# Attention of a two-layer kernel: scores made twice in 32-row tiles, the second time with the keys on partitions, against scores made once and transposed

## What is computed

```
q = (x @ wq).reshape(B, T, 2, 4, 128);  k_lat, v_lat = x @ wk_down, x @ wv_down      # 32 latent features a kv head
k = einsum('bkhl,ld->bkhd', k_lat, wk_up);  v = einsum('bkhl,ld->bkhd', v_lat, wv_up)
scores = einsum('bqhrd,bkhd->bhrqk', q, k) * scale
scores = where(causal, scores, lowest)
y = einsum('bhrqk,bkhd->bqhrd', softmax(scores), v)
out = y.reshape(B, T, 1024) @ wo
```

## Time and profile before

| | us |
|---|---|
| median of 3 runs | 2718.06 (2718.0 to 2718.55) |
| span of the profiled execution, first to last instruction | 2716.9 |
| PE busy in that span | 2138.8 (79%) |
| DVE busy | 1699.1 (63%) |
| ACT busy | 1440.2 (53%) |
| POOL busy | 1094.3 (40%) |
| mean granted TensorE clock | 0.861 |

### The profile page before, as it was taken

The page is one execution under the profiler, slowest core; times in us unless marked ns, Lnnn a source line. Parts: engine busy times, 40 slices in busy tenths (PEclk is TensorE's granted clock), DMA queues, the critical chain, the costliest instruction groups (busy, mean ns, idle before and its releaser), DMA issues.

```text
span 2716.9 us, 30658 instructions
## 1 busy us (share of the span) xinstructions
PE 2138.8 (79%) x8216; PEld 931.0 (34%) x8216; DVE 1699.1 (63%) x2749; ACT 1440.2 (53%) x2340; POOL 1094.3 (40%) x934
## 2 busy tenths in 40 slices
PE   5667887788778887788877888788877878778777
PEld 1201233343334333343333433333333433334344
DVE  1886458754688347882688646884477835877143
ACT  3342755647555565646556465554655556554352
POOL 0453146523465135550455323652346513554031
PEclk9556898898889987898888988889888989789898
DMA  5000000001000010000000000000100000000000
GB/s 162 15 20 8 12 12 13 16 6 24 1 13 16 6 24 12 17 5 12 12 13 16 6 15 9 13 16 6 24 5 17 8 8 21 13 13 5 0 1 4
DMA packets 55270, 41.95 MB, mean 15 GB/s; under 512 B 12672, under 2 KB 53264, under 8 KB 55056
## 3 DMA queue, kind: packets, MB, share of 16 engines
q1 hardware_dynamic: 50832, 37.41, 5.7%
q10 hardware_dynamic: 4224, 2.10, 0.3%
HBM read 12.21 MB, written 2.10 MB: 5 GB/s over the span
## 4 chain that ended last, share of the span: by engine, by line
PE 42%; issue 21%; DVE 20%; ACT 10%; POOL 5%; DVEq 1%; SPq 1%; ACTq 0%; POOLq 0%; DMA 0%
PE ps_g L636 15%; DVE sb_hst L1084 8%; PE ps_att L636 5%; PE ps_dt L540 5%; PE ps_y L587 4%; DVE sb_dbu L1077 3%; POOL sb_hc L1307 3%; PE ps_g L721 2%; POOL sb_h L1321 2%; PE ps_dt L575 2%; PE ps_du L540 2%; PE ps_g L713 2%; PE ps_att L733 2%; PE ps_du L569 1%; DVE sb_nmax L1195 1%
## 5 line engine op out<-in xcount | busy, mean ns | idle before, releaser
L1307 POOL TENSOR_TENSOR sb_hc<-sb_hst,sb_crep 128x512 f32<-128x512 f32 x512 | 654.2, 1279 | 743.5 <-DVE sb_hst L1084 743.5
L1084 DVE TENSOR_TENSOR_SCAN sb_hst<-ps_dt,sb_dbu 128x512 f32<-128x512 f32 x512 | 620.8, 1213 | 2.8 <-ACT ps_dt L854 1.4
L854 ACT ACTIVATE ps_dt<-ps_dt,sb_A 128x512 f32<-128x512 f32 x512 | 334.8, 660 | 404.6 <-PE ps_dt L575 403.1
L1077 DVE TENSOR_TENSOR sb_dbu<-ps_du,sb_brep 128x512 f32<-128x512 f32 x512 | 350.6, 685 | 233.5 <-PE ps_du L569 226.4
L575 PE MATMUL ps_dt<-sb_stk,sb_sel 96*128 96x512 bf16 x512 | 224.1, 438 | 100.4 <-DVE sb_hst L1084 97.3
L931 ACT ACTIVATE sb_h<-ps_g,sb_nmax 128x128 f32<-128x128 f32 (+3 forms) x256 | 134.8, 527 | 294.1 <-DVE sb_nmax L1195 262.0
L569 PE MATMUL ps_du<-sb_stk,sb_sel 96*128 96x512 bf16 x512 | 223.3, 436 | 68.1 <-DVE sb_dbu L1077 54.1
L1321 POOL TENSOR_TENSOR sb_h<-sb_h,sb_rz 128x128 f32<-128x128 f32 (+3 forms) x256 | 190.3, 746 | 185.4 <-DVE sb_rz L1199 173.1
L713 PE MATMUL ps_g<-sb_g,sb_qz 128*128 128x512 f32 (+3 forms) x512 | 222.2, 521 | 37.2 <-DVE sb_qz L1186 34.7
L1289 POOL TENSOR_TENSOR sb_tser<-sb_tser,sb_texp 128x512 f32<-128x512 f32 x32 | 40.5, 1265 | 495.5 <-ACT sb_tser L814 495.5
L721 PE MATMUL ps_g<-sb_const,sb_h 128*128 128x128 f32 x640 | 141.4, 326 | 122.5 <-POOL sb_h L1321 88.9
(11 more groups left out here) (249 smaller groups left out, 3594.3 us busy)
## 6 DMA issues: line engine op xcount, KB each, us to landing
sb_stk<-sb_parts SPq DMA_DIRECT2D x384, 64.0 KB, 2.0
sb_xtok<-in_L_attn_x_dram SPq DMA_DIRECT2D x8, 256.0 KB, 3.2
sb_ew<-in_L_ffn_w_dram SPq DMA_DIRECT2D x2, 1024.0 KB, 8.0
out_dram<-sb_lnv ACTq DMA_DIRECT2D x8, 256.0 KB, 2.5
sb_h<-in_L_ffn_h_w_dram SPq DMA_DIRECT2D x1, 1024.0 KB, 7.5
sb_g<-in_L_ffn_h_w_dram SPq DMA_DIRECT2D x1, 1024.0 KB, 8.8
sb_ew<-in_L_ffn_w_dram SPq DMA_DIRECT2D x8, 128.0 KB, 5.0
sb_hc<-in_L_attn_fw_convw_dram SPq DMA_DIRECT2D x1, 512.0 KB
```

The source lines that it names most:

```text
L854: act.activation(ps_dt[n % 2][:], ps_dt[n % 2][:], ACT.Exp, scale=A[d][:, g:g + 1]).then_inc(sem["dA"], 1)
L1077: dve.tensor_tensor(dbu[:, n % 2, :], ps_du[:], brep[n // NU][:], ALU.mult).then_inc(sem["dbu"], 1)
L1084: dve.tensor_tensor_scan(hst[:, n % 3, :], ps_dt[n % 2][:], dbu[:, n % 2, :], 0.0, ALU.mult, ALU.add).then_inc(sem["scan"], 1)
L1307: pool.tensor_tensor(hc[:, n % 6, :], hst[:, n % 3, :], crep[n // NU][:], ALU.mult).then_inc(sem["hc"], 1)
```

## The change

The head-by-head attention is replaced by one that works on pairs of heads, in two passes per sequence.

- **First pass**, 16 steps `s0` to `s15` (kv head, query tile t, pair): PE makes the scores of two heads, each a product over 32 rows (row tiles that start at partition 0, 32, 64 or 96), into the two banks of one pair of banks, and adds the mask to both. DVE takes the two heads' maxima in one reduction of 2x(t+1)*128 columns. The pairs of banks take turns. There is no `qz`, no exponential. After each eighth pair DVE splits the negated maxima into three bf16 parts (4 small operations on 128x16, `split`).
- **Between**, step `mT`: PE transposes the parts (4 bf16 transposes), ACT copies them to SBUF.
- **Second pass**, steps i = 0 to 17: for pair `e_i` (kv head, key tile j, pair) PE makes the scores again, with 128 keys on partitions and the (4-j)*128 queries along the row, two 32-row tiles; adds the negated maxima by a bf16 product over 32 rows (`pick`), and the mask. ACT makes one exponential of both heads, straight to SBUF. It is the operand of the values: no transposes, no copies. One step later `values(i-1)` makes, in four 32-column tiles, two products with `vlat` and two with a matrix of ones, which give the sums (`ps_z`). All `e_i` use the same pair of banks; `ps_att` and `ps_z` hold the other pair.
- **Normalisation** once per kv head (steps i = 9 and 17): ACT makes two Ln of 64 rows of `ps_z` and one Exp of the negative, DVE multiplies `ps_att` by it into `yT`. POOL has no part in the attention any more.
- `COST` gets entries for the new steps, so `FOLLOW` changes. The steps are 35 as before (26 to 60). Step 21 moves from slot 12 to 13. Slots 17 to 25 now hold s0,s1,s2 | s3,s4 | s5 | s6 | s7,s8,s9 | s10,s11 | s12,s13 | s14 | s15,mT, and slots 26 to 40 hold i = 0 | none | 1 | 2 | 3,4 | 5 | 6,7 | 8 | 9 | 10 | 11 | 12 | 13,14 | 15,16 | 17 with "ao" and its variance (these two were in slot 41).

```diff
+PAIRS = KV * TT * (REP // 2)
+def pair(i):
+    return i // (TT * REP // 2), i // (REP // 2) % TT, i % (REP // 2)
...
 PE:
+                def scores(i):
+                    k, t, p = pair(i)
+                    claim(f"s{i}")
+                    o = ps_pair[i % 2]
...
+                    for h, rows in heads(p):
+                        pe.matmul(o[:, h, 0:(t + 1) * P], qT[rows, k, t * P:(t + 1) * P], kT[rows, k, 0:(t + 1) * P],
+                                  start=True, stop=False)
+                    for h, _ in heads(p):
+                        ins = pe.matmul(o[:, h, t * P:(t + 1) * P], identb[:], maskb[:], start=False, stop=True)
+                def turned_scores(i):
+                    k, j, p = pair(i)
+                    claim(f"e{i}")
+                    o = ps_pair[0]
...
+                    for h, rows in heads(p):
+                        pe.matmul(o[:, h, j * P:T], kT[rows, k, j * P:(j + 1) * P], qT[rows, k, j * P:T],
+                                  start=True, stop=False)
+                    for h, rows in heads(p):
+                        pe.matmul(o[:, h, j * P:T], pick[rows, k, :], mT[rows, j * P:T], start=False, stop=False)
+                    for h, _ in heads(p):
+                        ins = pe.matmul(o[:, h, j * P:(j + 1) * P], maskb[:], identb[:], start=False, stop=True)
+                def values(i):
+                    k, j, p = pair(i)
+                    if i % (PAIRS // 2) == 0:
+                        claim(f"att{k}")
...
+                    for h, rows in heads(p):
+                        pe.matmul(ps_att[rows, j * P:T], vlat[:, j, k * LAT:(k + 1) * LAT],
+                                  pexp[i % 4][:, h, j * P:T], start=(j == 0), stop=(j == TT - 1))
+                    for h, _ in heads(1 - p):
+                        other = slice(LAT * (2 * (1 - p) + h), LAT * (2 * (1 - p) + h + 1))
+                        ins = pe.matmul(ps_z[other, j * P:T], ones[:], pexp[i % 4][:, h, j * P:T],
+                                        start=(j == 0), stop=(j == TT - 1))
+                for i in range(PAIRS):
+                    scores(i)
+                    yield
+                o = claim("mT")[:, 0:T // 2].bitcast(BF16)
+                pe.wait_ge(sem["split"], row("split", 2))
+                for t in range(TT):
+                    ins = pe.transpose(o[:, t * P:(t + 1) * P], nsplit[:, t, :, :].rearrange("p r c -> p (r c)"), identb[:])
+                for i in range(PAIRS + 2):
+                    if i < PAIRS:
+                        turned_scores(i)
+                    if 1 <= i <= PAIRS:
+                        values(i - 1)
+                    yield
...
 ACT:
+                act.activation(mT, full("mT")[:, 0:T // 2].bitcast(BF16), ACT.Copy).then_inc(sem["mT"], 1)
+                for i in range(PAIRS + 2):
+                    if i < PAIRS:
+                        act.activation(pexp[i % 4][:, :, j * P:T], ps_pair[0][:, :, j * P:T], ACT.Exp
+                                       ).then_inc(sem["pexp"], 1)
+                    if i in (PAIRS // 2 + 1, PAIRS + 1):
+                        k = pair(i - 2)[0]
+                        act.wait_ge(sem["att"], row("att", PAIRS // 2 * (k + 1)))
+                        for rows, other in ((slice(0, P // 2), slice(P // 2, P)), (slice(P // 2, P), slice(0, P // 2))):
+                            act.activation(logz[rows, :], ps_z[other, :], ACT.Ln).then_inc(sem["logz"], 1)
+                        act.wait_ge(sem["logz"], row("logz", 2 * k + 2))
+                        act.activation(rz[:], logz[:], ACT.Exp, scale=-1.0).then_inc(sem["rz"], 1)
...
 DVE:
+                    dve.tensor_reduce(nmax[:, k, t, 2 * p:2 * p + 2], ps_pair[i % 2][:, :, 0:(t + 1) * P], AX.X, ALU.max,
+                                      negate=True).then_inc(sem["smax"], 1)
+                    if i % (PAIRS // 2) == PAIRS // 2 - 1:
+                        split(k)
...
+                    if i in (PAIRS // 2 + 1, PAIRS + 1):
+                        dve.wait_ge(sem["rz"], row("rz", k + 1))
+                        dve.tensor_tensor(yT[:, k, :], ps_att, rz[:], ALU.mult).then_inc(sem["yT"], 1)
...
 COST:
-..., att0=0.9, att1=0.62, ...
+..., s0=0.7, s1=0.5, e0=1.2, e1=0.7, ...
-    rest += [w["att0"] + w["att1"] * head(min(j, HEADS * TT - 1))[1] for j in range(HEADS * TT + 3)]
+    rest += [w["s0"] + w["s1"] * pair(i)[1] for i in range(PAIRS)] + [w["ln"]]
+    rest += [w["e0"] + w["e1"] * (TT - 1 - pair(min(i, PAIRS - 1))[1]) for i in range(PAIRS + 2)]
```

More of the change, by code:

```diff
@@ L157, in rest_uses, with place @@
     return uses
-def place(uses, bank_of, before):
+def place(uses, banks_of, before):
     placed, last, i = {}, dict(before), 0
     for name, semaphore, count in uses:
-        bank = bank_of(i, name)
-        placed[name] = (bank, last[bank], i)
-        last[bank] = (semaphore, count)
+        banks = banks_of(i, name)
+        placed[name] = (banks, list(dict.fromkeys(last[bank] for bank in banks)), i)
+        last.update({bank: (semaphore, count) for bank in banks})
         i += name[:3] not in ("att", "sum")
@@ L383, in two_layer_kernel @@
         block = ctx.enter_context(nc.Block())
-        turn_banks = [bank[name] for name in ("g0", "g1", "g2", "att")]
+        turn_banks = [bank[f"g{i}"] for i in range(4)]
         def use(name):
-            return bank[(M_USE if name in M_USE else R_USE)[name][0]]
+            return bank[(M_USE if name in M_USE else R_USE)[name][0][0]]
         def first(name):
@@ L624, in claim @@
                 def claim(name):
-                    pe.wait_ge(sem[R_USE[name][1][0]], row(*R_USE[name][1]))
+                    for freed in R_USE[name][1]:
+                        pe.wait_ge(sem[freed[0]], row(*freed))
                     return use(name)
@@ L705, in rest, with heads @@
                 yield
+                def heads(p):
+                    return ((h, slice(LAT * (2 * p + h), LAT * (2 * p + h + 1))) for h in range(2))
                 def scores(i):
-                    k, t, r = head(i)
-                    o = claim(f"s{i}")
-                    if t == 0 and r == 0:
-                        pe.wait_ge(sem["kT"], row("kT", k + 1))
-                    pe.wait_ge(sem["qz"], row("qz", i + 1))
-                    pe.matmul(o[:, 0:(t + 1) * P], qz[:, r, :], kT[:, k, 0:(t + 1) * P], start=True, stop=False)
@@ L736, in values @@
[L736 to L744 removed]
+                    pe.wait_ge(sem["pexp"], row("pexp", i + 1))
+                    for h, rows in heads(p):
+                        pe.matmul(ps_att[rows, j * P:T], vlat[:, j, k * LAT:(k + 1) * LAT],
+                                  pexp[i % 4][:, h, j * P:T], start=(j == 0), stop=(j == TT - 1))
@@ new lines, in split @@
+                def split(k):
+                    m = nmax[:, k, :, :]
+                    hi, mid, lo = (nsplit[:, :, :, 2 * part + k] for part in range(3))
+                    dve.wait_ge(sem["smax"], row("smax", (k + 1) * PAIRS // 2))
+                    link(dve.tensor_copy(hi, m))
+                    link(dve.tensor_tensor(m, m, hi, ALU.subtract))
+                    link(dve.tensor_copy(mid, m))
+                    dve.tensor_tensor(lo, m, mid, ALU.subtract).then_inc(sem["split"], 1)
@@ new lines, in rest @@
+                for i in range(PAIRS):
+                    k, t, p = pair(i)
+                    dve.wait_ge(sem["full"], row("full", R_USE[f"s{i}"][2] + 1))
+                    dve.tensor_reduce(nmax[:, k, t, 2 * p:2 * p + 2], ps_pair[i % 2][:, :, 0:(t + 1) * P], AX.X, ALU.max,
+                                      negate=True).then_inc(sem["smax"], 1)
+                    if i % (PAIRS // 2) == PAIRS // 2 - 1:
+                        split(k)
+                    yield
+                yield
```

157 lines of the change are left out of this document (57 added, 100 removed).

## The result

The changed kernel takes 2847.52 us (median of 4 runs, 2847.29 to 2850.15), the kernel before 2718.31 beside it (4 runs, 2718.0 to 2719.41): ratio 1.0475, 95% interval [1.046, 1.049]. The forecast was 2707, its range ended at 2785. The profiled execution has a span of 2845.6 us and a mean PE clock of 0.800, against 2716.9 and 0.861.

The account below looks back on a forecast made before the run. Attention was taken as set by DVE and strict-order hand-overs between DVE, ACT, POOL and PE, not PE alone. 2716.9 - 22 (seven iterations of -3.2) + 11 (last sequence) = 2706, median 2707; own range 2685 to 2722, outer 2650 to 2785.

Parts of the forecast that it names:

- the one on the clock: PE's clock falls to 1.2 GHz after waits of over 6 us: +3.6 us per iteration, 3 in the last sequence.
- the first rival: More gain: PE's clock stays high in the denser second pass and DVE's stretched operations shrink: 2659 us, chance 0.17.
- T(n): PE's turned scores of a second-pass pair, n = 4-j: 1.46, 1.19, 0.91, 0.64 us for n = 4 to 1.
- V(n): PE's values products of a second-pass pair, n = 4-j: 0.22n + 0.1, that is 0.98 to 0.32 us.
- The chain: Table loads, two Ln and Exp on ACT, then DVE's product, at i = 9 and 17: 5.5 us each, uncovered.
- Slots 17 to 25: First pass in a steady iteration, paced by DVE: 39.5 us against 46.7 before.
- Slots 26 to 39: Second pass in a steady iteration, paced mostly by PE: 52.7 us against 57.3 before.
- The last sequence: Attention with no scan beside it: 62.3 us against 54.0 before, and 3 for the clock: +11.
- No overlap: Two row tiles on PE take the sum of both times instead of one: about 2798 us, chance 0.13.
- Bank pair: Second-pass scores wait for the previous exponential, 0.55 us exposed in 16 steps: +62, 2769 us; chance 0.20.
- Changes of tile shape: Switching PE tile shapes costs 0.15 us more in each of 16 second-pass steps: 2724 us, chance 0.10.
- slower: Chance 0.40 that the whole kernel ends slower than before, by more than the 0.2% (5.4 us) counted as same.

Follow-up runs that it names:

- run 1: The changed kernel with both passes' score products over all 128 rows, adding the other heads' scores (output not the reference's): 2801.65 us, ratio 1.0308.
- run 5: The kernel before with only its scores changed to 32-row products straight from qT, one head at a time, without `qz` and its copies: 2841.40 us, ratio 1.0459.
- run 7: The changed kernel with only the second pass's score products over all 128 rows (output not the reference's): 2863.63 us, ratio 1.0535.
- run 2: The changed kernel without the softmax's division: no Ln, no Exp of the sums, `yT` a plain copy of `ps_att`: 2742.53 us, ratio 1.0088.
- run 8: The changed kernel with both passes' scores over all 128 rows and no Ln/Exp division (output not the reference's): 2688.53 us, ratio 0.9883.
- run 6: The changed kernel with step 21 put back into slot 12, nothing else: 2848.14 us, ratio 1.0477.
- run 9: The changed kernel with 64-row score products, the other head's queries zeroed by two ACT copies, three exponential buffers instead of four: 3077.45 us, ratio 1.1319.
- run 11: run 9 with the first kv head's sums and outputs copied out, both divisions at the end, and two more steps before "ao": 3123.45 us, ratio 1.1488.
- run 4: The changed kernel with two bf16 filler products of 512 columns over 128 rows before each pair's scores, overwritten by them: 2897.47 us, ratio 1.0657.
- run 12: run 1 with the first kv head's sums and outputs copied out of the banks and both divisions at the end: 2786.38 us, ratio 1.0247.

## Why the prediction was wrong

**The step that failed** is the one on the clock: that it would fall after waits alone ("After a wait of over 6 us I expect V(8), T and V of slot 35 and part of "ao" at that level, +3.6 us"). With it went the first rival, by which denser work would keep the clock high. All of PE's terms T(n), V(n) and the first pass were priced at 2.4 GHz, and the stretches they fill were at 0.61 and 0.68. Every score of the kernel before is a product over 128 rows (`qz` is 32 rows of query among zeros), so its trace had no unbroken stretch of 32-row products to read the clock from. The drops that were read there stood behind waits, and that cause was taken for the only one. Runs 1, 5 and 7 show the other: with the number of PE instructions unchanged, the clock goes from 0.61 to 0.96 (run 1), from 0.78 to 0.53 (run 5), and in one pass while the other stays (run 7). Run 1 also ends the overlap of the heads and run 5 also leaves out copies; the height of the score products is what they share.

The Trainium skill ("TensorE: Matmul & The Clock Gate", the part on packing small matmuls) says that products in different row groups run at the same time; the trace agrees, with 0.97 us for two heads.

That overlap did not save time here: at 1.2 GHz two packed heads take 2.08 us, against 1.94 for the unpacked ones of run 1 at 2.4 GHz.

**The chain** was sized rightly: 5.5 us at two places and 3.6 for the clock behind it make 14.6 per sequence, 117 us in all; runs 2 and 8 measure 105 and 113, PE's list of waits 106. That nothing covers it held. From unit 40's drive to "ao" 7.4 us were said, with ACT's split copy and exponential ahead of the chain, and it took 7.4: from 1165.75 to 1173.14.

**Slots 17 to 25**: 42.1 for 39.5. At a clock of 0.96 it is 38.4 (run 1), so the count by DVE was right to 1.1 us and the rest is the clock.

**Slots 26 to 39**: 66.4 for 52.7. Without the chain 57.3 (run 2) and at full clock, with doubled streaming, 54.2 (run 8). The forecast less its chain (5.5 us) and the exponential ahead of it (1.1) is 46.1, and of the 8.1 between them the second head's streaming can be all (0.22n over 16 pairs is 8.8): the counts for full clock were near the truth. T(4) at full clock is right (1.46 said; 0.97 to L748, 0.31 to the masks and 0.22 for them, 1.50), the maxima too (103.2/8 = 12.9 us against 13.3). The pace of the whole is PE at 1.2 GHz: slots 35 and 36 took 5.1 and 7.8 us for 2.6 and 5.6. (Slot 37, 5.5 for 4.6, takes 5.5 in run 1 too; there the count was short.) An estimate for the whole iteration at full clock: run 1's 327.7 less those 8.8 is 318.9, 1.2 above the forecast.

**Slots 0 to 16**: 65.5 for 63.3. The prediction put nothing there, though one step moved (run 6).

**The last sequence**: +34 for +11. Its waits before L761 and "ao" were 6.30 and 4.53 us, near the count; the other 23 us come with a clock of 0.58 through both passes.

**The rivals.** No overlap: refuted (0.97 us for two). Bank pair: PE's idle time before the turned scores is 7.3 us over the whole span (the group above), against the 62 of the rival; with PE fast again it is 17.3 in run 1, still no 62. Changes of tile shape: at full clock T is as counted. The sign came from none of the mechanisms that were listed: the 0.40 given to "slower" rested on others.

## What to carry to other kernels

Before row tiles are packed to save PE's time, look at what else lives on PE's clock: here the packed products and their neighbours (the spreading, the reduction) ran at 1.2 GHz and lost more than the packing saved, and copying queries into zeros, on an engine with room, was the cheaper form by 123 us (run 5). Read the granted clock of a window beside the shape of its products, not only beside its gaps. And a Ln, Exp, product chain between two stages that PE runs in order costs its full length each time; a price taken from one column or one shape (the reciprocal's 0.16 us) says nothing of 512 columns.

## What the hardware did that was not expected

- The granted clock followed the height of the score products, not PE's busy share: 0.61 at 86% busy with 32 rows, 0.96 at 79% with 128, 0.62 at 93% with 64 rows (the changed kernel, run 1, one iteration of run 9; slots 17 to 25). The lowest, 0.51, was with PE 96% busy (run 11).
- Zeros in the operand did not lower it: with 96 of 128 rows at zero the kernel before has 0.78, with the same 32 rows alone it has 0.53 (run 5).
- It fell within unbroken work, between 2701.1 and 2702.0 in the rows above. In the 12 us of 32-row products ahead of that the clock was up and no wait was longer than 0.57 us; run 1 has a wait of 0.70 us there and stays up.
- bf16 products over 128 rows between them lifted it from 0.61 to 0.87 (run 4).
- DVE's reciprocal took 3.36 us for 64 rows of 512 columns, where ACT's Ln of the same shape took about 0.6.

Left open: no version here that computes the whole attention is faster than the kernel before. Full height without the other heads' scores needs zeros in one operand only, and that can be a 128-column tile, as `qz` was: the queries' tile in the first pass, the keys' in the second. That form was not tried, and run 12 (2786), which adds the other heads' scores, is the nearest to it. Run 8 (2688) is about what it would take with both chains hidden, before the copies into the zeros are paid. In every run with short products PE also changes between products of different height, so what the changes alone do to the clock is not shown.
